# One tile list per expert, full tiles first, in an attention and top-2 expert kernel

## The chip, the cores and the metric

The kernel runs on one core of a Trainium2 chip. The metric is the device time of one execution in microseconds (us), the median of several runs. Engine names as in the profile: PE (TensorE), DVE (VectorE), ACT (ScalarE), POOL (GpSimd) and SP (SyncE, which here only issues DMAs).

## The reference, cut to what matters

```
x   = x + attention(layernorm(x), ctx)   # 16 batches x 128 rows, D = 128, 16 heads of 8, then Wo
h   = layernorm(x)                       # 2048 rows
p   = softmax(h @ wg.T)                  # 8 experts
w,i = top_k(p, 2);  w = w / sum(w)
y_e = (silu(h @ w1_e.T) * (h @ w3_e.T)) @ w2_e.T      # 256 hidden columns, fp32
out = x + sum over the two chosen experts of w * y_e
```

All is fp32. 2048 rows with two experts each make 4096 pairs (row, expert). How many pairs an expert gets is known only once the kernel has routed the rows.

## The kernel before, in words

The 16 batches are worked on in four quartets of four batches (512 rows). Attention of the quartets runs until about 180 us. As soon as the rows of a quartet are finished, they are normalised a second time and routed (`routing_step`, `place_rows` on DVE, small matmuls `fill(("x2T", q))`, `lg`, `rk`, `cn` on PE). `place_rows` writes into `rows_i` the place of every pair in a DRAM buffer `xg`, which has one region per expert. POOL then **sends** the quartet: eight indirect DMAs of 128 rows (L970, `send`), with the pair's number as a 129th column. A send waits for the send of the batch before it with the same k, so at most two are under way.

Then comes the expert stage, a loop over tiles of 128 pairs of one expert. For tile n, SP reads the rows from `xg` (L458, ring of XR = 15 buffers), PE turns them (L680), ACT and DVE split them into a high and a low part (L761, L1341), PE multiplies by w1 and w3 (`hidden`, L693 to L696), ACT and DVE make silu and product (L922, L1375), PE turns the result (L706), ACT and DVE split it (L761, L1346), PE multiplies by w2 (`down`, L719 and L720), DVE adds the two halves into `y_sb` (`take_rows`, L1353, ring of YR = 14), and POOL **scatters** the tile's rows to their pairs' places in the DRAM buffer `ys` (L1009). Every engine has its part of iteration n written out by hand in one fixed order, so an engine that waits holds up all that stands behind it in its own list. On PE and DVE the work of tile n + 1 (turning, split) stands ahead of `hidden(n)`, and `down` and `take_rows` come three iterations behind.

Which expert and which rows a tile has is read from a table `tab`, made on DVE (`table`) and loaded into registers by SP (`open_phase`, L441) and PE (`columns`, L730). The list of tiles has a fixed length, enough for the worst split. Rows between an expert's last pair and the end of its last tile are **pads**: nine DMAs of 128 rows (L435, L439) write them, and their number is out of range, so a scatter drops them.

There are two phases, each with its own regions, `ys` buffer, pads and table: quartets 0 to 2 with 31 tiles, and quartet 3 with 15. Phase 1 can't open until the last quartet has been routed, its table made and its eight sends landed. That happens inside the loop of phase 0: the last batch's heads in iterations 0 to 2, its statistics and normalisation in 3 and 4, routing on DVE in 8 to 11, the table in 13 to 15, and on POOL one send after every second scatter from n = 8 to 22. POOL's scatter n waits until scatter n - 2 has landed (up to n = 39).

SP's list in the loop: read n waits for the turning of tile n - 15 and for the landing of scatter n - 15; ahead of read 31 stands `open_phase(1)`. After the reads SP waits for all scatters of phase 0, brings the results of quartets 0 to 2 back (L468, six DMAs of 256 KB), waits for those of phase 1, brings back the last quartet (L475, four of 128 KB), and writes the output. DVE's `gather` (L1362, L1363) weighs the two results of each row and adds them to x; gathers 0 to 5 stand in the last six tile iterations, 6 to 15 after the loop.

## Time and profile before

| | us |
|---|---|
| median of 3 runs (298.17 to 303.82) | 299.11 |
| the profiled execution, its own time | 301.1 |
| its span in the trace | 299.3 |
| PE busy (share of the span) | 225.5 (75%) |
| DVE busy | 219.7 (73%) |
| ACT busy | 139.2 (47%) |
| POOL busy | 114.3 (38%) |

Times inside the trace count from the start of the span. The profiled execution took 1.8 us more than its span, and 2.0 more than the median. A busy share is an average over attention and the expert stage, which have different limits; the chain of waits tells which wait ends last at each moment. POOL's busy time for a DMA is only the issuing (0.97 us for an indirect one); the transfer lands later.

### The profile page before, as it was taken

What the parts mean: (1) busy time and instruction counts of PE and PEld (TensorE: products, weight loads), DVE (VectorE), ACT (ScalarE), POOL (GpSimd) and SP (SyncE); (2) the same over time, 40 slices, a digit from 0 to 9 for tenths busy, and PEclk for the clock granted to TensorE, in tenths of its full rate; (3) what the DMA queues carried; (4) which work ended last, traced back from release to release, by engine and by line L of the source; (5) the groups of instructions that cost most, each with busy time, mean ns of one, the idle gap of its engine ahead of it and who ended that gap; (6) DMA issues with size and microseconds to landing.
All of it is one profiled execution on the core that took longest, in us unless ns stands there. A gap on an engine that the chain in (4) does not pass through costs nothing.

```text
span 299.3 us, 5642 instructions
## 1 busy us (share of the span) xinstructions
PE 225.5 (75%) x1522; PEld 171.6 (57%) x1522; DVE 219.7 (73%) x636; ACT 139.2 (47%) x312; POOL 114.3 (38%) x125
## 2 busy tenths in 40 slices
PE   0666888999899789795678664886889983999700
PEld 0643565667566557563366333775869973898500
DVE  5689965886688777969776831788788880788963
ACT  6684156655764474331445461543345550555300
POOL 5202150405030521053863540055367656443650
PEclk9996599999999999788557965999799996899965
DMA  7954513451344124426021333212123344253107
GB/s 214 339 189 99 132 29 79 94 115 34 70 98 82 35 47 93 83 59 208 10 63 45 68 76 83 58 31 73 37 68 88 81 84 102 64 157 103 37 11 211
DMA packets 40862, 27.31 MB, mean 91 GB/s; under 512 B 5214, under 2 KB 38501, under 8 KB 40448
## 3 DMA queue, kind: packets, MB, share of 16 engines
q1 hardware_dynamic: 37440, 20.95, 29.7%
q0 software_dynamic: 2816, 5.27, 5.9%
q10 hardware_dynamic: 576, 0.72, 0.8%
q8 instruction: 14, 0.23, 0.3%
q14 instruction: 16, 0.13, 0.2%
HBM read 13.27 MB, written 7.37 MB: 69 GB/s over the span
## 4 chain that ended last, share of the span: by engine, by line
PE 41%; DVE 22%; DMA 17%; SPq 8%; issue 7%; POOL 2%; ACT 1%; POOLq 1%; DVEq 0%
SPq L413 7%; PE bank L500 7%; DVE m_neg L1317 5%; DMA ys<-big 5%; DMA xg<-st_hi,rows_i 4%; DMA bd<-st 3%; PE bank L693 3%; PE bank L640 3%; PE bank L719 3%; PE bank L619 3%; PE bank L657 3%; PE bank L643 3%; PE bank L696 3%; PE bank L694 3%; PE bank L506 2%
## 5 line engine op out<-in xcount | busy, mean ns | idle before, releaser
L1009 POOL DMA_INDIRECT ys<-big x46 | 45.2, 982 | 38.3 <-DMA ys<-big 18.3
L1317 DVE TENSOR_REDUCE m_neg<-bank 128x4 f32<-128x512 f32 x64 | 43.3, 683 | 15.6 <-PE bank L657 15.2
L887 ACT ACTIVATE big<-bank 128x512 f32<-128x512 f32 x64 | 37.5, 597 | 23.5 <-PE bank L643 23.3
L761 ACT ACTIVATE st<-bank 128x128 fp32r<-128x128 f32 (+1 forms) x92 | 26.3, 329 | 35.3 <-PE bank L706 19.6
L970 POOL DMA_INDIRECT xg<-rows,rows_i x24 | 24.0, 1000 | 27.5 <-DVE rows_i L1173 12.4
L657 PE MATMUL bank<-bd,st 128*128 128x512 f32 x64 | 29.6, 499 | 6.4 <-DMA bd<-st 5.2
L640 PE MATMUL bank<-m_bd,ones_b 128*128 128x512 f32 x64 | 32.2, 504 | 2.4 <-ACT big L887 1.9
L1263 DVE SCALAR_TENSOR_TENSOR st<-st_hi,cst,bank 128x512 fp32r<-128x512 f32 x32 | 23.4, 748 | 9.2 <-ACT st_hi L761 4.5
L719 PE MATMUL bank<-bd,st 128*128 x92 | 27.5, 320 | 2.3 <-DVE big L1353 2.1
L987 POOL TENSOR_TENSOR m_bd<-mT,cst 128x512 fp32r<-128x512 f32 x16 | 17.2, 1109 | 30.1 <-DVE mT L1242 30.1
L922 ACT ACTIVATE big<-bank 128x256 f32<-128x256 f32 x46 | 17.7, 385 | 22.0 <-PE bank L696 21.8
L643 PE MATMUL bank<-bd,st 128*128 128x512 f32 x64 | 27.8, 434 | 0.0
L1375 DVE TENSOR_TENSOR big<-big,bank 128x256 f32<-128x256 f32 x46 | 19.3, 419 | 11.4 <-ACT big L922 11.2
L953 POOL TENSOR_SCALAR ve<-mv 128x4 f32<-128x4 f32 x8 | 1.8, 228 | 66.2 <-DVE mv L1040 66.2
L693 PE MATMUL bank<-bd,st 128*128 x46 | 23.7, 515 | 3.1 <-DVE st L1341 2.8
L720 PE MATMUL bank<-bd,st 128*128 x92 | 24.7, 290 | 0.0
L1341 DVE TENSOR_TENSOR st<-bank,st 128x128 fp32r<-128x128 f32 x46 | 13.0, 283 | 13.1 <-ACT st L761 12.9
L680 PE MATMUL bank<-cst,big 128*128 128x128 f32 x46 | 13.7, 298 | 11.0 <-DMA big<-xg 11.0
L657 PEld LDWEIGHTS bank<-bd,st 128*128 128x128 f32 x64 | 14.1, 227 | 13.7 <-issue 6.6
L1346 DVE TENSOR_TENSOR st<-bank,st 128x256 fp32r<-128x256 f32 x46 | 19.4, 422 | 2.7 <-ACT st L761 1.4
L719 PEld LDWEIGHTS bank<-bd,st 128*128 128x128 f32 x92 | 18.1, 197 | 5.1 <-issue 3.5
L1353 DVE TENSOR_REDUCE big<-bank 128x128 f32<-128x256 f32 x46 | 19.2, 418 | 1.2 <-PE bank L720 1.0
(159 smaller groups left out, 538.0 us busy)
## 6 DMA issues: line engine op xcount, KB each, us to landing
bd<-st SPq DMA_DIRECT2D x128, 64.0 KB, 2.0
big<-xg SPq DMA_DIRECT2D x46, 64.5 KB, 1.9
raw<-in_L_ffn_w SPq DMA_DIRECT2D x2, 1024.0 KB, 9.0
raw<-ys SPq DMA_DIRECT2D x6, 256.0 KB, 4.6
xg<-in_patterns SPq DMA_DIRECT2D x18, 64.5 KB, 3.4
x_all<-in_x SPq DMA_DIRECT2D x4, 256.0 KB, 3.9
rows<-in_mask_BxS_if POOLq DMA_DIRECT2D x4, 256.0 KB, 4.9
ctx_all<-in_L_ffn_w SPq DMA_DIRECT2D x1, 1024.0 KB, 6.0
```

The source lines that it names most:

```text
L640: nc.tensor.matmul(s2[k % 2][:, :], ones_b[:, b, :], m_bd[:, NJ * g:NJ * (g + 1), :].rearrange("p h q -> p (h q)"), start=True, stop=False)
L643: nc.tensor.matmul(s2[k % 2][:, :], st[:, (u - 1) % 2, 1, g, b * S:(b + 1) * S], bd_slot(0, n)[:, g, :, :].rearrange("p j q -> p (j q)"), ...
L657: nc.tensor.matmul(s1[k % s1_ring(u)][:, :], st[:, u % 2, 0, g, (b - 1) * S:b * S], bd_slot(1, n)[:, g, :, :].rearrange("p j q -> p (j q)" ...
L693: nc.tensor.matmul(both, t_lo[n % 2], first_high[:, :, bass.ds(col[n], I)], start=True, stop=False)
L719: nc.tensor.matmul(o, g_hi[n % GR][:, c * P:(c + 1) * P], w, start=(c == 0), stop=False)
L720: last = nc.tensor.matmul(o, g_lo[n % GR][:, c * P:(c + 1) * P], w, start=False, stop=(c == 1))
L761: return nc.scalar.activation(o, i, ACT.Copy)
L887: nc.scalar.activation(prob[n % 2][:, NJ * g:NJ * (g + 1), :].rearrange("p h q -> p (h q)"), s2[k % 2][:, :], ACT.Exp, scale=SCALE).then_i ...
L970: pool.indirect_dma_start(xg[f], bass.IndirectOffsetOnAxis(rows_i[:, n, k:k + 1], 0), sent_rows(n // QB)[:, n % QB, k, :], None, bounds_ch ...
L1009: pool.indirect_dma_start(ys[f], bass.IndirectOffsetOnAxis(xt[n % XR][:, D:RW].bitcast(I32), 0), y_sb[n % YR], None, bounds_check=2 * CAPS ...
L1263: nc.vector.scalar_tensor_tensor(st[:, u % 2, is_k, g, :], st_hi[:, n % SH, :].bitcast(F32), cst[:, (C_CK if is_k else C_CQ):(C_CK if is_k ...
L1317: nc.vector.tensor_reduce(m_neg[:, H * (b - 1) + NJ * g:H * (b - 1) + NJ * (g + 1)], s1[k % s1_ring(u)][:, :].rearrange("p (j q) -> p j q" ...
```

## The change

All four quartets go to one list per expert: one `xg` with one region per expert, one `ys`, one running count. The list has 39 tiles in all. A tile is full once 128 pairs of its expert are there; three quartets have 3072 pairs, of which at most 127 in each of 8 experts are left over, so at least 17 full tiles exist before the last quartet is routed. These 17 are the first part of the list (`full_tiles`). The other 22 (`other_tiles`) are in two groups per expert: first, expert by expert, the tiles that the first three quartets have begun and that are not among the 17, then the tiles that only the last quartet fills. The results of quartets 0 to 2 are complete after tile 31 (`FIRST_TILES`).

Moved: `open_phase(1)`, with the only nine pads that are left, stands ahead of read 17 on SP; the first opening has no pads. The last batch's heads and its statistics stand ahead of the loop; normalisation is in iteration 0, routing in 4 to 6 and 8, the second table in 10 to 12 (with twice as many groups). A fourth part of the first table is new on DVE (tick 15 of the last attention block). POOL sends the last quartet in one row after scatter 3. Scatter n waits for scatter n - 2 up to tile 16, for n - 4 from 17 on. All 16 gathers stand behind the loop.

```diff
@@ -55,12 +55,13 @@
 EPS = 1e-5
 SH = 3
 CT = 128
-PHASES = (3, NQ - 3)
-CAPS = [n * T for n in PHASES]
-NTS = [(2 * c - E) // CT + E for c in CAPS]
-NT = sum(NTS)
-NC = CAPS[0] // CT
-REGS = [c + CT for c in CAPS]
+ROUTED = 2 * (NQ - 1) * T
+FULL_TILES = (ROUTED - E * (CT - 1) + CT - 1) // CT
+FIRST_TILES = (ROUTED - E) // CT + E
+NT = (2 * B * S - E) // CT + E
+NTS = (FULL_TILES, NT - FULL_TILES)
+NC = B * S // CT
+REG = B * S + CT
...
-            def open_phase(f):
-
-                sp.wait_ge(pad_ready, f + 1)
-                sp.dma_start(xg[f][E * REGS[f]:E * REGS[f] + CT, :], consts[:, C_PAD:C_PAD + RW]).then_inc(padded[f], 16)
-                _, at = nc.values_load_multi_w_load_instructions(pad[0:1, f, :], [mybir.EngineType.SP], min_val=0, max_val=E * REGS[f] - CT,
+            def fill_pads():
+
+                sp.wait_ge(pad_ready, 1)
+                sp.dma_start(xg[E * REG:E * REG + CT, :], consts[:, C_PAD:C_PAD + RW]).then_inc(padded, 16)
+                _, at = nc.values_load_multi_w_load_instructions(pad[0:1, :], [mybir.EngineType.SP], min_val=0, max_val=E * REG - CT,
                                                                  skip_runtime_bounds_check_because=IN_RANGE)
                 for row in at:
-                    sp.dma_start(xg[f][bass.ds(row, CT), :], consts[:, C_PAD:C_PAD + RW]).then_inc(padded[f], 16)
+                    sp.dma_start(xg[bass.ds(row, CT), :], consts[:, C_PAD:C_PAD + RW]).then_inc(padded, 16)
+
+            def open_phase(f):
+
+                if f:
+                    fill_pads()
                 sp.wait_ge(tab_ready, f + 1)
-                _, at = nc.values_load_multi_w_load_instructions(tab[0:1, 0, 32 * f:32 * f + NTS[f]], [mybir.EngineType.SP],
-                                                                 min_val=0, max_val=E * REGS[f], skip_runtime_bounds_check_because=IN_RANGE)
+                _, at = nc.values_load_multi_w_load_instructions(tab[0:1, 0, NTS[0] * f:NTS[0] * f + NTS[f]], [mybir.EngineType.SP],
+                                                                 min_val=0, max_val=E * REG, skip_runtime_bounds_check_because=IN_RANGE)
                 for q in (range(3) if f == 0 else range(3, NQ)):
                     for k in range(2):
                         sp.wait_ge(sent[q][k], 16 * QB)
-                sp.wait_ge(padded[f], 16 * (E + 1))
+                if f:
+                    sp.wait_ge(padded, 16 * (E + 1))
                 return list(at)
 
             rows = open_phase(0)
             sp.wait_ge(o_full, 3 * QB)
             for n in range(NT):
-                f = int(n >= NTS[0])
                 if n == NTS[0]:
                     rows += open_phase(1)
                 if n >= XR:
...
-            results_back(0)
+            results_back(FIRST_TILES)
...
-            results_back(1)
+            results_back(NT)
...
+            heads_by_query(B - 1)
+            heads_by_dim(B - 1)
+            project_out(B - 1)
...
-                if n < 3:
-                    (heads_by_query, heads_by_dim, project_out)[n](B - 1)
-                if n == 5:
+                if n == 1:
                     fill(("x2T", NQ - 1))
-                if n == 7:
+                if n == 3:
                     fill(("lg", NQ - 1))
-                if n == 10:
+                if n == 6:
                     fill(("rk", NQ - 1))
-                if n == 12:
+                if n == 8:
                     fill(("cn", 1))
...
-                f = int(n >= NTS[0])
-                if 2 <= n < NT - 6:
-                    pool.wait_ge(ysb_out[(n - 2) % YR], 16 * ((n - 2) // YR + 1))
-                pool.indirect_dma_start(ys[f], bass.IndirectOffsetOnAxis(xt[n % XR][:, D:RW].bitcast(I32), 0), y_sb[n % YR], None,
-                                        bounds_check=2 * CAPS[f] - 1, oob_is_err=False).then_inc(ysb_out[n % YR], 16)
-                if n == 8:
-                    pool.wait_ge(rows_ready, NQ)
-                if 8 <= n < 8 + 4 * QB and n % 2 == 0:
-                    send(QB * (NQ - 1) + (n - 8) // 4, n // 2 % 2)
+                back = 2 if n < NTS[0] else 4
+                if n >= back:
+                    pool.wait_ge(ysb_out[(n - back) % YR], 16 * ((n - back) // YR + 1))
+                pool.indirect_dma_start(ys, bass.IndirectOffsetOnAxis(xt[n % XR][:, D:RW].bitcast(I32), 0), y_sb[n % YR], None,
+                                        bounds_check=PAIRS - 1, oob_is_err=False).then_inc(ysb_out[n % YR], 16)
+                if n == 3:
+                    send_quartet(NQ - 1)
...
+                if part == 3:
+                    own(nc.vector.tensor_tensor(until[:, :], until[:, :], tiles[:, :], ALU.subtract))
+                    own(nc.vector.tensor_scalar(until[:, :], until[:, :], -1.0, float(n), ALU.mult, ALU.add))
+                    own(nc.vector.scalar_tensor_tensor(tiles[:, :], until[:, :], 0.0, tiles[:, :], ALU.max, ALU.min))
+                    tiles_of(begun[:, :], 0, 3 * T // CT, ALU.is_gt)
+                    own(nc.vector.tensor_tensor(group[:, 0, :], begun[:, :], tiles[:, :], ALU.subtract))
+                    own(nc.vector.scalar_tensor_tensor(origin[:, 0:E], tiles[:, :], float(CT), base, ALU.mult, ALU.add))
+                    own(nc.vector.scalar_tensor_tensor(origin[:, E:2 * E], begun[:, :], float(CT), base, ALU.mult, ALU.add))
+
+            def other_tiles(part):
+
+                n = NTS[1]
+                number = cst[:, C_TILE:C_TILE + n]
+                groups = group[:, :, :].rearrange("p k e -> p (k e)")
+                below = x2s[1][:, 0:4 * E * E].rearrange("p (m f) -> p m f", f=2 * E)
+                passed, moved = (x2s[k][:, 0:n * 2 * E].rearrange("p (n m) -> p n m", m=2 * E) for k in range(2))
+                spot, column = (line[:, k * n:(k + 1) * n] for k in range(2))
+                if part == 0:
+                    counts(1)
+                    nc.vector.tensor_tensor(pad[:, :], cnt[:, :], base, ALU.add).then_inc(pad_ready, 1)
+                    tiles_of(tiles[:, :], 0, NC, ALU.is_gt)
+                    own(nc.vector.tensor_tensor(group[:, 1, :], tiles[:, :], begun[:, :], ALU.subtract))
+                    own(nc.vector.tensor_tensor(below, groups.unsqueeze(1).to_broadcast([P, 2 * E, 2 * E]), upto, ALU.mult))
+                    own(nc.vector.tensor_reduce(ended[:, 1:2 * E + 1], below, X, ALU.add))
+                if part == 1:
+                    own(nc.vector.scalar_tensor_tensor(origin[:, :], ended[:, :], -float(CT), origin[:, :], ALU.mult, ALU.add))
+                    own(nc.vector.tensor_tensor(step[:, :], origin[:, 1:2 * E + 1], origin[:, 0:2 * E], ALU.subtract))
+                    own(nc.vector.tensor_tensor(passed, ended[:, 1:2 * E + 1].unsqueeze(1).to_broadcast([P, n, 2 * E]),
+                                                number.unsqueeze(2).to_broadcast([P, n, 2 * E]), ALU.is_le))
+                    own(nc.vector.tensor_tensor(moved, passed, step[:, :].unsqueeze(1).to_broadcast([P, n, 2 * E]), ALU.mult))
+                    own(nc.vector.tensor_reduce(spot, moved, X, ALU.add))
+                if part == 2:
+                    own(nc.vector.tensor_tensor(moved, passed, cst[:, C_STEP:C_STEP + 2 * E].unsqueeze(1).to_broadcast([P, n, 2 * E]), ALU.mult))
+                    own(nc.vector.tensor_reduce(column, moved, X, ALU.add))
+                    own(nc.vector.tensor_copy(tab[:, 1, NTS[0]:NT], column))
+                    own(nc.vector.scalar_tensor_tensor(spot, number, float(CT), spot, ALU.mult, ALU.add))
+                    nc.vector.tensor_scalar(tab[:, 0, NTS[0]:NT], spot, origin[:, 0:1], float(E * REG), ALU.add, ALU.min).then_inc(tab_ready, 1)
...
-                                table(0, tick - 9)
+                                full_tiles(tick - 9)
                             if tick == 12:
                                 weigh(2)
+                            if tick == 15:
+                                full_tiles(3)
...
+            normalise_heads(B - 1)
+            take_projection(B - 1)
+            second_statistics(NQ - 1)
             rest_of_tile(0)
             for n in range(NT + 3):
                 if n + 1 < NT:
...
                 if n == 0:
-                    normalise_heads(B - 1)
-                if n == 2:
-                    take_projection(B - 1)
-                if n == 3:
-                    second_statistics(NQ - 1)
-                if n == 4:
                     normalise(QB * (NQ - 1), 2 * NQ - 1)
-                if 8 <= n < 11:
-                    routing_step(NQ - 1, n - 8)
-                if n == 11:
+                if 4 <= n < 6:
+                    routing_step(NQ - 1, n - 4)
+                if n == 6:
+                    routing_step(NQ - 1, 2)
+                if n == 8:
                     place_rows(NQ - 1)
-                if 13 <= n < 16:
-                    table(1, n - 13)
-                if NT - 5 <= n < NT + 1:
-                    gather(n - NT + 5)
-
-            for b in range(6, B):
+                if 10 <= n < 13:
+                    other_tiles(n - 10)
+
+            for b in range(B):
```

What the change moves, as lists of instructions per engine. First **POOL** in the expert stage, before: L1009 is a scatter (`ys<-big`), L970 a send (`xg<-rows,rows_i`).

```order
L954 TENSOR_TENSOR rstd<-ve,halves 128x4
L1009 DMA ys<-big 3072x128 x9
L970 DMA xg<-rows,rows_i 5248x129
L1009 DMA ys<-big 3072x128 x2
...
L1009 DMA ys<-big 3072x128 x8
L1009 DMA ys<-big 1024x128 x15
```

POOL now (L1019 scatters, L980 sends):

```order
L965 TENSOR_TENSOR rstd<-ve,halves 128x4
L1019 DMA ys<-big 4096x128 x4
L980 DMA xg<-rows,rows_i 17536x129 x8
L1019 DMA ys<-big 4096x128 x35
L172 UNCONDITIONAL_BRANCH
```

The eight sends were spread over scatters 8 to 22; they now stand together between scatters 3 and 4.

**DVE** ahead of the loop's first tiles, now (L1125 to L1119 heads of the last batch, L1043 and L1048 its statistics, L1066 and L1069 its normalisation, L1398, L1435 and L1403 tile work); before, the first rows were the tile work, and the others stood in iterations 0 to 4:

```order
L1125 RECIPROCAL rz<-bank 128x16
L1128 TENSOR_TENSOR on<-bank,rz 128x128
L1119 TENSOR_TENSOR x_all<-bank,x_all 128x128
L1043 BN_STATS stats<-x_all 128x6 x4
L1048 BN_AGGR mv<-stats 128x2 x4
L1398 TENSOR_TENSOR st<-bank,st 128x128 x2
L1435 TENSOR_TENSOR big<-big,bank 128x256
L1066 CAST rows<-cst 128x8
L1069 TENSOR_SCALAR rows<-x_all,mv,rstd 128x2x128 x4
L1398 TENSOR_TENSOR st<-bank,st 128x128
```

The heads and statistics now precede the split of tile 0, and the normalisation stands right behind the first product.

**DVE** at the end of the loop, before (L1353 adds up a tile's result, L1362 and L1363 are a gather):

```order
L1353 TENSOR_REDUCE big<-bank 128x128
L1346 TENSOR_TENSOR st<-bank,st 128x256
L1362 SCALAR_TENSOR_TENSOR big<-raw,wgt,x_all 128x128
L1363 SCALAR_TENSOR_TENSOR ctx_all<-raw,wgt,big 128x128
L1353 TENSOR_REDUCE big<-bank 128x128 x2
L1362 SCALAR_TENSOR_TENSOR big<-raw,wgt,x_all 128x128
```

and now (L1410 adds up, L1419 and L1420 are a gather):

```order
L1410 TENSOR_REDUCE big<-bank 128x128
L1403 TENSOR_TENSOR st<-bank,st 128x256
L1410 TENSOR_REDUCE big<-bank 128x128 x2
L1419 SCALAR_TENSOR_TENSOR big<-raw,wgt,x_all 128x128
L1420 SCALAR_TENSOR_TENSOR ctx_all<-raw,wgt,big 128x128
```

The six gathers that stood between tiles have moved behind the last tile.

## Rows read from the trace of the kernel before

**Rows 1.** The view of `ys`: scatters' durations (ns), POOL's idle (us, times), landings.

```profile
L1009 POOL DMA_INDIRECT ys<-big x46: 969/971/1193, 195.7 to 288.6; - x46
...
  issue: 6.7, 21
...
DMA to landing us min/median/max: 2.1/2.6/7.0
```

**Rows 2.** Chain of waits, 240 to 250 us: start, length, what.

```profile
240.85 4.05 DMA ys<-big
...
247.02 2.35 DMA xg<-rows,rows_i
...
249.56 1.90 DMA big<-xg
```

**Rows 3.** Timeline of PE: start, length, instruction, idle before it and releaser.

```profile
184.77 0.79 PE L693 MATMUL bank<-bd,st 128*128 x1
...
222.44 0.49 PE L693 MATMUL bank<-bd,st 128*128 x1 [0.61 <-DVE st L1341]
...
251.51 0.48 PE L680 MATMUL bank<-cst,big 128*128 128x128 f32 x1 [5.89 <-DMA big<-xg]
251.86 0.79 PE L693 MATMUL bank<-bd,st 128*128 x1
...
260.17 0.49 PE L693 MATMUL bank<-bd,st 128*128 x1
...
263.42 0.48 PE L693 MATMUL bank<-bd,st 128*128 x1
...
278.82 0.49 PE L693 MATMUL bank<-bd,st 128*128 x1
```

**Rows 4.** Chain of waits at the end.

```profile
288.61 2.10 DMA ys<-big
...
291.31 2.94 DMA raw<-ys
...
294.34 0.36 DVE big L1362
```

**Rows 5.** The third quartet's sends: first on POOL's timeline, two later in the chain.

```profile
165.04 1.26 POOL L970 DMA_INDIRECT xg<-st_hi,rows_i  x1 [2.13 <-DVE rows_i L1173]
...
168.46 4.40 DMA xg<-st_hi,rows_i
...
178.96 2.29 DMA xg<-st_hi,rows_i
```

**Rows 6.** SP's pads on its timeline; then register loads of SP and PE by source line.

```profile
236.10 5.45 SPq L439 DMA_DIRECT2D xg<-in_patterns  x8
...
L441 SPq TENSOR_LOAD <-tab x2: 1537/1974/2411, 173.5 to 241.6; - x2
L730 PEldq TENSOR_LOAD <-tab x2: 1723/2322/2922, 178.0 to 252.7; - x2
```

**Rows 7.** DVE's timeline: heads, normalisation, places and one table step.

```profile
178.66 0.29 DVE L1109 TENSOR_TENSOR x_all<-bank,x_all 128x128 f32<-128x128 f32 x1 [1.88 <-PE bank L530]
...
195.57 1.57 DVE L1061 TENSOR_SCALAR rows<-x_all,mv,rstd 128x256 f32<-128x256 f32 x4
...
215.04 0.25 DVE L1173 CAST rows_i<-m_hl 128x8 int32<-128x8 f32 x1
...
220.77 0.27 DVE L1206 TENSOR_TENSOR ck<-until,cst 128x120 f32<-128x120 f32 x1
```

**Rows 8.** POOL's timeline: scatters, with the idle time before each.

```profile
260.29 0.97 POOL L1009 DMA_INDIRECT ys<-big  x1 [0.96 <-DMA ys<-big]
...
263.49 0.97 POOL L1009 DMA_INDIRECT ys<-big  x1 [0.94 <-DMA ys<-big]
```

**Rows 9.** DVE's timeline after the loop: two gathers in succession.

```profile
288.03 0.35 DVE L1362 SCALAR_TENSOR_TENSOR big<-raw,wgt,x_all 128x128 f32<-128x128 f32 x1
...
288.68 0.35 DVE L1362 SCALAR_TENSOR_TENSOR big<-raw,wgt,x_all 128x128 f32<-128x128 f32 x1
```

More of the change, by code:

```diff
@@ L312, in program @@
         pad_ready = sem("pad_ready")
-        padded = [sem(f"padded{k}") for k in range(2)]
+        padded = sem("padded")
         in_t = [sem(f"in_t{k}") for k in range(XR)]
@@ L1182, in weigh, with counts @@
                 own(nc.vector.tensor_reduce(wgt[:, QB * q:QB * (q + 1), :], spread[:, :, :, :], X, ALU.add))
-            def table(f, part):
-                n = NTS[f]
-                upto = cst[:, C_UPTO:C_UPTO + E * E].rearrange("p (e f) -> p e f", e=E)
+            upto = cst[:, C_UPTO:C_UPTO + 4 * E * E].rearrange("p (m f) -> p m f", f=2 * E)
+            base = cst[:, C_BASE:C_BASE + E]
+            def counts(f):
+                full(("cn", f))
+                nc.vector.tensor_copy(cnt[:, :], work_bank(("cn", f))[:, 0:E]).then_inc(into_sbuf(("cn", f)), 1)
+                taken(dve, ("cn", f))
@@ new lines, in tiles_of, with full_tiles @@
+            def tiles_of(out_tiles, first, last, compare):
+                c = last - first
+                need = x2s[0][:, 0:E * c].rearrange("p (e f) -> p e f", e=E)
+                own(nc.vector.tensor_tensor(need, cnt[:, :].unsqueeze(2).to_broadcast([P, E, c]),
+                                            cst[:, C_FULL + first:C_FULL + last].unsqueeze(1).to_broadcast([P, E, c]), compare))
+                own(nc.vector.tensor_reduce(out_tiles, need, X, ALU.add))
+            def full_tiles(part):
+                n = NTS[0]
```

93 lines of the change are left out of this document (45 added, 48 removed).

## The prediction

> **What bounds the kernel now.** I read the windows of the second half first (everything up to about 180 us stays, but for one small piece), then the chain of waits, then PE, POOL, SP and DVE in order of time. The expert stage starts with tile 0 at 184.77 and ends its last tile's start at 278.82 [rows 3]: 94.05 us for 45 steps. Undisturbed, a step is (263.42 - 260.17) / 2 = 1.625 us [rows 3], so 45 steps are 73.1 and 21 us are something else. One piece is the 5.89 us in which PE waits for a read of phase 1 at 251.51, followed by matmuls of 0.79 instead of 0.49 us: from 251.86 to 260.17 four steps took 8.3 instead of 6.5, 1.8 more [rows 3]. The longer duration is the lower of the two clocks (1.2 for 2.4 GHz) after an idle PE. The chain shows what that wait was for: scatters and sends that wait for one another's landings (4.05, then the last send, 2.35), then the read (1.90) [rows 2]. The rest, 13 us, is the last quartet's heads, statistics, routing and table between the tiles. Behind tile 45 come 20.5 us: three iterations, POOL's remaining scatters until 288.61, a landing of 2.10, the results' way back (2.94), four gathers and the output from 294.34 to 299.3 [rows 4]. So the stage is bound by the tile loop, with POOL's queue behind it at both ends.
>
> **The change, part by part.** I follow landmarks in the time of this trace.
>
> *Start of tile 0.* Two edits pull against each other. The nine pads no longer run beside the third quartet's sends. These took 165.04 to 178.96 + 2.29 = 181.25, 16.2 us, with one landing of 4.40 [rows 5]; four rounds of 2.3 to 2.6 plus 0.8 to issue the next would be 13.6. Reads could start 2.6 earlier. Against that, heads and statistics of the last batch and PE's register load (between 1.7 and 2.9 [rows 6], 1.9 for 17) now stand ahead of tile 0. They can't start before batch 14 is taken at 178.66 [rows 7]; the fourth table part ahead of it (eight small operations, estimated at 1.8, some of it in idle time) moves that to about 180.2. Two short DVE operations, three on PE, one on ACT and DVE's addition, each 0.3 to 0.8, make about 2.7 (an estimate from such rows as the 0.29 at 178.66), and the register load 1.9, then the split of tile 0: 185.0, that is **+0.2**. Ends: -2.5 (all of it hidden) and +1.8 (the table part wholly exposed and nothing gained).
>
> *Last quartet's rows.* Before, normalisation ended at 195.57 + 1.57 = 197.1 and `rows_i` was written at 215.3 [rows 7], 18.2 later over seven iterations. Now there are eight: 19.8. Normalisation follows tile 0's product (about 2.4 behind 185.0) and takes 1.7, so it ends at 189.1 and the rows are there at **208.9**.
>
> *PE at the second opening.* Tiles 0 to 16 took 222.44 - 184.77 = 37.7 [rows 3]. Off goes the statistics' 1 us. The second table now is wholly ahead of tile 16, and bigger. An operation on 120 elements took 0.27, one on 256 a quarter of 1.57 [rows 7]; on 22 x 16 = 352 elements I take 0.5, times five, plus some fourteen small ones: 5.9 us for the three parts, about 2.2 more than stood ahead of tile 16 before. PE is ready for tile 16 at 185.0 + 37.7 + 1.2 = **223.9**; ahead of it stands the turning of tile 17.
>
> *Second opening.* It needs three things. The sends in a row: first issue 208.9 + 0.8, and a row of 16.2 like the third quartet's, which also had nine pads beside it: 225.9. The other end is 13.6 (223.3); I take the upper, since the pads are there again. The pads: ready at 212.5, 1.9 for the first and the registers, 5.45 for eight [rows 6], all issued at 219.9. The table: four iterations and 4.7 behind the rows, 220.1, and SP's load of 22 numbers, 1.9 (1.54 for 15, 2.41 for 31 [rows 6]): 222.0. The sends decide. Issue and landing of read 17, 0.4 and 1.9 [rows 2]: 228.2. **PE waits 4.3** instead of 5.9, in another place, and what the idle PE costs afterwards in clock stays at 1.8 [rows 3]; the other end for it is 0.
>
> *Last tile.* Tile 16 starts at 228.4; 22 steps of 1.625 and 1.8: tile 38 starts at **265.9**. So the stage up to the last tile's start is 80.9 instead of 94.05. Of these 13.1, seven steps fewer are 11.4, the shorter stall 1.6, statistics and bigger table -1.2; the remaining 1.3 are what stood between tiles behind tile 16 and no longer does, the end of the table and the gathers. On PE, scatters 4 to 16 also have to be landed for reads 19 to 31; at the paces below they are, with some 3 us to spare.
>
> *POOL.* Blocked by the sends, it issues scatter 4 at 223.6 + 1.3 = 224.9. With a wait two back the pace is (263.49 - 260.29) / 2 = 1.6 [rows 8]: scatter 17 at 245.7. From there four may be under way, so only issuing counts, 0.97 and 6.7 / 21 = 0.3 [rows 1]: 21 more end at 272.8. The six loads of results come in meanwhile; the worst landing before was 7.0 [rows 1]; with four outstanding this costs 7.0 + 0.8 - 5.1, 2.7 at most, 0 at least, and I take 0.7. Scatter 38 at 273.5, landed 275.8, 0.6 + 2.94 back [rows 4]: 279.3.
>
> *DVE.* Tile 38's result is added up some 5.3 behind its start, 271.2. Twelve gathers of 0.65 [rows 9] and the weights, 0.8, now follow instead of standing between tiles: 279.8. That is the later one, by a hair. Four gathers and the output, 299.3 - 294.34 = 5.0 [rows 4]: the span ends at **284.8**, 14.5 less.
>
> The profiled execution took 301.1, the median is 299.11; minus 14.5 they give 286.6 and 284.6. I say **285**.
>
> The Trainium skill's page "DMA: Bandwidth & Descriptors" (Anatomy of one DMA, SWDGE path) prices a DMA from GpSimd at 2.0 us and bytes over 436 GB/s, 2.15 for 64 KB; by that estimate the row of sends would be about 12.3 and the time that of the first rival. This trace's landings of 2.29, 2.35, 4.05 and 4.40 agree with it only where nothing else is under way.
>
> **Rivals.** *1, the stall nearly goes.* The row takes 13.6: read 17 lands at 225.6, PE idles 1.7 and keeps its clock. POOL's end is 2.6 earlier, the tiles' 4.4; POOL decides, 276.7 + 5.0 = 281.7, on the median **281.5**. For it: no scatters run beside the row. Against: the pads do. Chance 0.20.
>
> *2, the stall only moves.* If rows or sends come 3 to 6 us later (routing in the first, slow-clocked iterations, more landings like 4.40), each microsecond counts once, for PE and POOL alike: **288 to 291**. Chance 0.20.
>
> *3, DVE holds up POOL.* The first send of the third quartet took 1.26 instead of 0.97 [rows 1, 5], while DVE was busy. If all eight in the row did, beside DVE's new table, that is 8 x 0.29 = 2.3: **287**. For it: more two-input DVE work stands beside this row than before. Against: the median of the scatters, 0.971, issued amid DVE's tile work. Chance 0.08. The Trainium skill's page "SBUF — State Buffer" (Who interferes with whom) has the rule: a DVE instruction with two SBUF inputs and a GpSimd one that reads SBUF block each other.
>
> *4, slower: landings set POOL's pace.* In the row four landings follow one another, and with a wait two back each scatter costs half of landing + 0.8. One us more per landing costs 4 in the row and 6.2 in scatters 4 to 16, 10 us in all, with 3 us of slack to PE and none to the end. The gain is used up at landings 1.4 longer than I assume (3.8 for scatters, 4.5 for sends); at 2.1 longer it is **306**. For it: 4.05 and 4.40 occur [rows 2, 5]. Against: the median is 2.6 [rows 1], and they occurred beside pads. Chance 0.04; short of it, between 293 and 305, 0.08.
>
> That the list does not open early is excluded by the code: `open_phase(1)` stands ahead of read 17, and 17 is what three quartets guarantee.
>
> **How the numbers follow.** My forecast, 282.5 to 288, has 0.40. What a measurement can tell is about 2%, 6 us: faster is below 293.1, slower above 305.1. Faster: 0.40 + 0.20 + 0.20 + 0.08 = 0.88; within 2%: 0.08; slower: 0.04. The range of 8 in 10 reaches from rival 1 with the start's lower end to rival 2's upper end, **279 to 291**.
>
> **What would show it.** Right: 39 tiles; eight sends in a row for some 16 us from about 209; one idle of PE of some 4 us ahead of tile 16 and none later; the last scatter within 1 us of the last gather before the results' wait. The start is wrong if tile 0 is not near 185; the rows' landmark if `rows_i` is not near 209; the POOL part if reads 19 to 31 make PE wait, or if DVE waits over 1 us for the last results. The whole is wrong if POOL's scatters end after 278.

## The result and the profile after

| | before | after |
|---|---|---|
| median, us | 298.97 (four runs, 298.17 to 303.82) | 290.14 (four runs, 289.75 to 291.26) |
| profiled execution: time, span | 301.1, 299.3 | 290.28, 288.5 |
| tile 0, tile 16, last tile (PE) | 184.77, -, 278.82 | 186.91, 230.20, 268.14 |
| idle PE at the second opening | 5.89 | 3.20 |

The ratio is 0.972 (95% interval 0.968 to 0.976): 8.8 us faster, where 14 were forecast. The time lies inside the range of 279 to 291, at its upper end, and outside the forecast's own 282.5 to 288. The profile after was taken on a run at its median; the one before on a run 2.1 us above it. So 10.8 us of span are 8.8 of median. Here and below, medians are of all runs of a set, while ratios and intervals leave out its slow runs (more than 1.5% above the fastest of their kernel), so the two can differ a little.

PE's timeline, which answers to [rows 3] (start, length, instruction, idle before it and releaser):

```profile
185.69 0.66 PE L691 MATMUL bank<-cst,big 128*128 128x128 f32 x2 [3.71 <-issue]
186.91 0.79 PE L704 MATMUL bank<-bd,st 128*128 x1 [0.56 <-DVE st L1398]
...
217.17 0.49 PE L704 MATMUL bank<-bd,st 128*128 x1 [1.64 <-DVE st L1398]
220.53 0.49 PE L704 MATMUL bank<-bd,st 128*128 x1 [1.53 <-DVE st L1398]
223.40 0.49 PE L704 MATMUL bank<-bd,st 128*128 x1 [1.04 <-DVE st L1398]
...
229.97 0.48 PE L691 MATMUL bank<-cst,big 128*128 128x128 f32 x1 [3.20 <-DMA big<-xg]
230.20 0.79 PE L704 MATMUL bank<-bd,st 128*128 x1
```

Two things are new. Ahead of tile 0 PE is idle for 3.71 us for "issue", so for nothing that another engine owes it. And tiles 12 to 14 wait for DVE, which makes the bigger table meanwhile; that cost nothing here, since the idle time ahead of tile 16 follows. The source lines of the register loads say what the issue was (they answer to [rows 6]; durations in ns, then first and last start):

```profile
L452 SPq TENSOR_LOAD <-tab x2: 1492/3114/4736, 169.9 to 223.1; - x2
...
L744 PEldq TENSOR_LOAD <-tab x2: 1883/3062/4240, 181.4 to 231.1; - x2
```

PE's load of 17 numbers at 181.4 took 4.24 us, its load of 22 at 231.1 only 1.88; on SP it is the load of 22 that was long, 4.74. On the chain of waits the first shows as issue behind read 0's landing, the second by its name:

```profile
180.66 1.84 DMA big<-xg
182.51 3.18 issue
185.69 0.46 PE bank L691
...
222.84 0.25 DVE tab L1271
223.10 4.74 SPq L452
228.13 1.79 DMA big<-xg
229.97 0.48 PE bank L691
```

POOL's row of sends (it answers to [rows 5]), and the scatter behind it:

```profile
211.65 0.96 POOL L980 DMA_INDIRECT xg<-rows,rows_i  x1 [7.33 <-DVE rows_i L1183]
...
220.65 0.97 POOL L980 DMA_INDIRECT xg<-rows,rows_i  x1 [1.71 <-DMA xg<-rows,rows_i]
224.14 0.97 POOL L980 DMA_INDIRECT xg<-rows,rows_i  x1 [2.51 <-DMA xg<-rows,rows_i]
225.47 0.97 POOL L980 DMA_INDIRECT xg<-rows,rows_i  x1 [0.36 <-issue]
226.74 0.97 POOL L1019 DMA_INDIRECT ys<-big  x1 [0.30 <-issue]
```

First to last issue is 13.82 us; in the other runs read 17 is issued 2.5 us behind the last send (but for the seven more tiles below, where SP's load is longer still), which here would be 227.95. SP's load ended at 227.84: a tie. The end, which answers to [rows 4, 9], on DVE and on POOL:

```profile
274.65 0.42 DVE L1410 TENSOR_REDUCE big<-bank 128x128 f32<-128x256 f32 x1 [1.48 <-PE bank L731]
275.00 0.34 DVE L1419 SCALAR_TENSOR_TENSOR big<-raw,wgt,x_all 128x128 f32<-128x128 f32 x1
...
283.26 0.22 DVE L1192 TENSOR_REDUCE wgt<-spread 128x8 f32<-128x64 f32 x1
283.51 0.35 DVE L1419 SCALAR_TENSOR_TENSOR big<-raw,wgt,x_all 128x128 f32<-128x128 f32 x1
```

```profile
274.43 0.97 POOL L1019 DMA_INDIRECT ys<-big  x1 [0.95 <-DMA ys<-big]
276.52 0.97 POOL L1019 DMA_INDIRECT ys<-big  x1 [1.12 <-DMA ys<-big]
```

DVE goes from the last sum to the last gather without a gap; it no longer waits for results. POOL has caught up with the tiles: its last scatter leaves 1.45 us behind the end of the last sum (275.07), and the profile puts the wait ahead of it down to the landing of an earlier scatter.

### The profile page after: what moved, and what is told of

Same layout as the page of the kernel before. It is cut to its first block, busy times and chain, and to the rows that moved or that the text cites. A ratio compares the mean times of both kernels' runs of the same rounds, so it can differ in the third digit from the quotient of the medians.

```text
span 288.5 us, 5277 instructions
## 1 busy us (share of the span) xinstructions
PE 214.9 (75%) x1445; PEld 162.2 (56%) x1445; DVE 214.6 (74%) x619; ACT 132.5 (46%) x291; POOL 107.7 (37%) x118
## 4 chain that ended last, share of the span: by engine, by line
PE 49%; DVE 27%; DMA 9%; issue 7%; SPq 4%; ACT 2%; POOL 1%; DVEq 0%; POOLq 0%; ACTq 0%
PE bank L511 7%; DVE m_neg L1374 5%; PE bank L630 4%; PE bank L730 4%; PE bank L651 4%; DMA xg<-st_hi,rows_i 4%; PE bank L668 4%; PE bank L654 3%; PE bank L704 3%; PE bank L707 3%; DMA bd<-st 3%; PE bank L731 3%; PE bank L517 3%; PE bank L705 3%; SPq L419 2%
## 5 line engine op out<-in xcount | busy, mean ns | idle before, releaser
L1374 DVE TENSOR_REDUCE m_neg<-bank 128x4 f32<-128x512 f32 x64 | 43.4, 684 | 15.7 <-PE bank L668 15.5
L1019 POOL DMA_INDIRECT ys<-big x39 | 38.2, 980 | 32.1 <-DVE big L1410 15.8
L899 ACT ACTIVATE big<-bank 128x512 f32<-128x512 f32 x64 | 37.5, 597 | 24.2 <-PE bank L654 24.0
L980 POOL DMA_INDIRECT xg<-rows,rows_i x24 | 23.9, 996 | 39.3 <-DVE rows_i L1183 18.9
L773 ACT ACTIVATE st<-bank 128x128 fp32r<-128x128 f32 (+1 forms) x78 | 22.5, 329 | 32.0 <-PE bank L717 16.8
L1435 DVE TENSOR_TENSOR big<-big,bank 128x256 f32<-128x256 f32 x39 | 16.3, 419 | 12.1 <-ACT big L935 12.1
L730 PE MATMUL bank<-bd,st 128*128 x78 | 23.8, 324 | 1.9 <-DVE big L1410 1.9
L935 ACT ACTIVATE big<-bank 128x256 f32<-128x256 f32 x39 | 15.0, 386 | 21.2 <-PE bank L707 21.0
L704 PE MATMUL bank<-bd,st 128*128 x39 | 20.2, 519 | 5.3 <-DVE st L1398 5.3
L668 PEld LDWEIGHTS bank<-bd,st 128*128 128x128 f32 x64 | 14.1, 228 | 13.9 <-issue 6.9
L731 PE MATMUL bank<-bd,st 128*128 x78 | 21.7, 297 | 0.0
L651 PEld LDWEIGHTS bank<-m_bd,ones_b 128*128 128x128 f32 x64 | 13.9, 218 | 10.2 <-issue 5.9
L630 PE MATMUL bank<-big 128*32 128x128 f32 x512 | 19.2, 296 | 0.0
L1403 DVE TENSOR_TENSOR st<-bank,st 128x256 fp32r<-128x256 f32 x39 | 16.5, 422 | 3.4 <-ACT st L773 2.5
L730 PEld LDWEIGHTS bank<-bd,st 128*128 128x128 f32 x78 | 15.9, 204 | 4.5 <-issue 3.5
L1410 DVE TENSOR_REDUCE big<-bank 128x128 f32<-128x256 f32 x39 | 16.3, 418 | 2.5 <-PE bank L731 2.4
```

Source lines behind the costliest of these rows:

```text
L630: last = nc.tensor.matmul(ob[n % 2][R * j:R * (j + 1), half * P:(half + 1) * P], va[(n // QB) % 2][:, ((n % QB) * 4 + half * 2 + i) * NJ + ...
L651: nc.tensor.matmul(s2[k % 2][:, :], ones_b[:, b, :], m_bd[:, NJ * g:NJ * (g + 1), :].rearrange("p h q -> p (h q)"), start=True, stop=False)
L668: nc.tensor.matmul(s1[k % s1_ring(u)][:, :], st[:, u % 2, 0, g, (b - 1) * S:b * S], bd_slot(1, n)[:, g, :, :].rearrange("p j q -> p (j q)" ...
L704: nc.tensor.matmul(both, t_lo[n % 2], first_high[:, :, bass.ds(col[n], I)], start=True, stop=False)
L730: nc.tensor.matmul(o, g_hi[n % GR][:, c * P:(c + 1) * P], w, start=(c == 0), stop=False)
L731: last = nc.tensor.matmul(o, g_lo[n % GR][:, c * P:(c + 1) * P], w, start=False, stop=(c == 1))
```

## The experiments

The sets of four ran on three chips, on which the kernel before took 299.35, 311.74 and 301.25 us; so each run is compared with its own set, by ratio to the kernel before, or by landmarks of its trace.

### What a tile costs: seven more

```
-NT = (2 * B * S - E) // CT + E
+NT = (2 * B * S - E) // CT + E + 7
```

> The changed kernel with NT raised by 7, so that the list has 46 tiles again; the seven extra ones hold no rows. Theory A (the tile loop bounds the stage): seven steps of 1.62 us and a table of 29 instead of 22 columns (+0.4 us on VectorE) come on top: 290.1 + 11.8 = 301.9 us, tile 16 at +0.4. Rival B (GpSimd's queue bounds the second half): the extra scatters cost its undisturbed pace, 1.28 us each, 290.1 + 9.0 = 299.1 us. Rival C (full tiles cost more than empty ones because of their transfers): under 297 us.

Measured 311.07 us, ratio 1.040 (1.034 to 1.046): 20.8 us more, far over each theory. The loads show why:

```profile
L744 PEldq TENSOR_LOAD <-tab x2: 4238/5720/7203, 182.3 to 233.9; - x2
```

29 numbers took PE 7.20 us between tiles 16 and 17, and SP 6.10. On PE that is 8.4 us from tile 16 to tile 17 instead of 3.1, 5.3 more. On SP the load ended at 230.6, and read 17, issued at 230.94, came 2.3 later than the last send (226.13) and its 2.5 would have let it. More tiles make a longer row of `tab`, so its second row starts elsewhere. I wrote the bytes from the start of `tab` beside every load so far. Long: 156 and 184 (17 numbers, 4.24 and 4.24), 68 (22 and 29, 4.74 and 6.10), 252 (29, 7.20). Short: 0, 128, 192, 224 and 320 (15 to 31 numbers, 1.5 to 2.9, all loads of the kernel before among them). So before the change every load of `tab` began on a multiple of 32 bytes from its start, and after it two of four don't.

### The start: load ahead, and the old schedule

```
+            col = columns(0)
             heads_by_query(B - 1)
             heads_by_dim(B - 1)
             project_out(B - 1)
...
-            col = columns(0)
             turn_tile(0)
```

> TensorE loads its 17 registers ahead of the last batch's heads (about 178.9 us) instead of behind them (181.4). Theory A (the 4.24 us come from what runs beside the load, SyncE's fifteen reads being issued from 180.66): here it takes 1.5 to 1.9 us, tile 0 starts near 184.6 instead of 186.9 and the time is 287.8 us. Rival B (a load of 17 numbers takes TensorE over 4 us by itself): the heads come 4.2 us later, tile 0 stays near 187, 290.1 us or up to 1 us more.

Measured 289.54 us, ratio 0.970 (0.963 to 0.976); the load took 4.32 us from 178.2, 2.3 us before the first read was issued (180.54), and tile 0 started at 187.51. Rival B: the reads beside it are not the cause. Nor is the count alone, as the table's layout shows below.

The second experiment puts `heads_by_query`, `heads_by_dim` and `project_out` back into iterations 0 to 2 and the rest of the last quartet into those of the kernel before (cut to two of the moved parts):

```
-                if n == 8:
+                if n == 11:
                     place_rows(NQ - 1)
-                if 10 <= n < 13:
-                    other_tiles(n - 10)
+                if 13 <= n < 16:
+                    other_tiles(n - 13)
```

> The list of 39 tiles and everything else of the changed kernel, but the last quartet's heads, statistics, routing and table at the iterations they had before (heads in 0 to 2, normalisation in 4, routing 8 to 10, rows in 11, table 13 to 15). Theory A: tile 0 starts 2 to 3 us earlier (near 184.3), the rows three iterations later (4.9) less that start, so rows near 213 and the idle time ahead of tile 16 near 5.5 instead of 3.2 us; 290.1 + 2.2 = 292.3 us. Rival B (the start is all that counts, the second opening has room): 287.5 us. Rival C (the table's end stands ahead of tile 16 and everything slips): 295 us or more.

Measured 293.77 us, ratio 0.982 (0.980 to 0.984). Tile 0 at 184.36, as expected: there the long load (4.34 us, from 178.7) is over at 183.0, about when read 0 has landed. But the first send came at 217.50 instead of 211.65, and PE then waited 11.45 us ahead of tile 16, at 235.85, where 5.5 were expected. Theory A had the start right and the rows 3.7 us too early (near 213, measured 216.7); the time lies between A and C. So the earlier schedule of the change is worth 3.0 us by the ratios (3.6 by the medians), through the rows.

### The row of sends, moved

```
-                if n == 3:
+                if n == 9:
                     send_quartet(NQ - 1)
```

> The row of the last quartet's eight sends stands behind scatter 9 instead of scatter 3; GpSimd waited 7.33 us for rows_i ahead of the row, and scatters 4 to 9 fit in there. Theory A (behind the row GpSimd has slack; its last scatter waits for the last tile's result): no change, 290.1 us within 0.6, while the scatters' backlog behind the row ends some 8 us earlier. Rival B (the backlog of scatters holds reads or the results' way back): 287 to 288 us. Rival C (a landing of scatter 8 or 9 delays the first send): the idle time ahead of tile 16 grows by 1 to 1.3 us, 291.3 us.

Measured 297.67 us, ratio 0.995 (0.990 to 0.999): none of the three. I had not looked when scatter 9 can be issued: it needs tile 9's result. It went out at 223.33, so the row began 12.95 us later and tile 16 started 9.83 later. That is the clearest miss among my expectations, and the clearest proof that the row sets tile 16; that `rows_i` sets the row is shown by the experiment ahead of this one. The difference, 3, is the row itself. In this run the pads were over before it, on SP and POOL:

```profile
218.01 6.11 SPq L445 DMA_DIRECT2D xg<-in_patterns  x8
```

```profile
224.60 0.97 POOL L980 DMA_INDIRECT xg<-rows,rows_i  x1 [0.30 <-issue]
...
235.52 0.97 POOL L980 DMA_INDIRECT xg<-rows,rows_i  x1 [0.57 <-issue]
```

10.92 us from first to last issue instead of 13.82, so the pads beside the row are put at 2.9. Only this run has the last quartet's row without them, but the twelve other traces of the new list, all with pads beside it, have 12.67 to 14.24. The third quartet's row, which lost its pads by the change, went from 13.92 to 11.91.

### The table's layout alone

```
-        tab = sb("tab", [P, 2, NT], I32)
+        tab = sb("tab", [P, 2, 64], I32)
...
-tab[0:1, 1, NTS[0] * f:NTS[0] * f + NTS[f]]
+tab[0:1, 1, 32 * f:32 * f + NTS[f]]
```

(Parts of the changed lines; the same for row 0 and where DVE writes it.)

> Only the layout of the table tab changes: rows of 64 words, the second list from word 32, so that each of the four register loads begins at a multiple of 128 bytes from the start of tab; before this edit they begin at bytes 0 (17 numbers, 1.49 us), 68 (22 numbers, 4.74), 156 (17, 4.24) and 224 (22, 1.88). Theory A (where a register load begins sets its price, about 0.07 us a number on such a boundary and 0.21 to 0.25 off it): SyncE's second load takes 1.9 us, TensorE's first one 1.5 to 1.8; tile 0 starts near 184.6 instead of 186.9; behind the second opening the sends' landing decides in place of the load, and the shift of the start stays: 290.1 - 2.3 = 287.8 us. Rival B (the loads are long through what runs beside them, reads being issued at one, sends at the other): they stay at 4.2 and 4.7 us, and the time at 290.1. Rival C (the loads get short, but the row of sends holds everything): tile 0 earlier, idle time ahead of tile 16 longer by as much, 290.1.

Measured 295.55 us on the chip that took 311.74 for the kernel before: ratio 0.950 (0.937 to 0.962). Source lines, then PE:

```profile
L452 SPq TENSOR_LOAD <-tab x2: 1495/1558/1622, 169.6 to 219.7; - x2
...
L744 PEldq TENSOR_LOAD <-tab x2: 1566/1724/1883, 181.1 to 228.0; - x2
```

```profile
226.88 0.48 PE L691 MATMUL bank<-cst,big 128*128 128x128 f32 x1 [3.49 <-DMA big<-xg]
227.07 0.79 PE L704 MATMUL bank<-bd,st 128*128 x1
```

4.24 became 1.57 and 4.74 became 1.62, with as many numbers loaded at the same places in the program. Tile 0 started at 183.91 (3.0 earlier) and tile 16 at 227.07 (3.1 earlier). At the second opening the chain now goes through the last send (222.62) and its landing, so SP's shorter load brings nothing of its own. Theory A holds by the loads and by tiles 0 and 16, with a start 0.7 better than expected. From tile 16 to tile 38 this trace took 46.9 us instead of 37.9, so it ran once more on another chip:

> The aligned kernel once more, on another chip, since the chip of its first timing gave 311.7 us for the kernel before instead of 299. In that trace TensorE's first load took 1.57 and SyncE's second 1.62 us, tile 0 started at 183.91 instead of 186.91 and tile 16 at 227.07 instead of 230.20. Theory A (these 3.0 to 3.1 us stay to the end): 290.1 - 3.1 = 287.0 us, ratio to the kernel before 0.960. Rival B (from tile 17 on transfers set the pace, 1.72 us a step in that trace, and take the gain back): 289 us or more, steps over 1.65 us on this chip too.

Measured 286.51 us, ratio 0.951 (0.946 to 0.956), clear of the changed kernel's 0.968 to 0.976. Loads 1.56 and 1.63, tile 0 at 185.98 with read 0 issued 1.8 later than in the profile after (180.66); from read 0's issue to tile 0 it is 3.5 instead of 6.3. Tile 16 started at 228.45, 1.75 earlier than in the profile after, and from there to tile 38 it took 38.0. By the ratios this version beats both kernels, and it is 14.7 us under the 301.25 of its own set. Theory A was nearest, but its ratio of 0.960 lies above the interval: between 0.972 and 0.951 are some 6 us, of which the landmarks show about half, and the rest has no cause on record. The "1.72 us a step" of my expectation was misread: the first trace's steps were about 1.6, but for a few behind gaps, told of at the end.

### Where a load may begin

```
+            for first, count in ((0, 17), (1, 17), (2, 17), (4, 17), (8, 17), (16, 17), (0, 8), (1, 8), (0, 30), (3, 29)):
+                nc.values_load_multi_w_load_instructions(tab[0:1, 1, first:first + count], ...)
```

> The aligned kernel, with ten more register loads on TensorE behind its last product, whose values nobody uses: 17 numbers from words 0, 1, 2, 4, 8 and 16 of a row of tab, 8 numbers from words 0 and 1, 30 from word 0 and 29 from word 3. Theory A (the start address decides): 17 numbers take 1.5 to 1.9 us from words 0, 8 and 16 and about 4.2 from words 1, 2 and 4; 8 numbers 0.6 and 2.0; 30 from word 0 2.3 to 2.9 and 29 from word 3 about 7. Rival B (number and neighbours decide): equal counts take equal times here, where nothing else runs. Rival C (some other boundary, of 8 or 16 bytes): word 2 or 4 are short too.

It told nothing of this: the ten loads do not appear in the trace, presumably removed because nobody uses them. One run of the aligned kernel remains, 286.23 us. Which boundary counts stays open: all short starts, 224 among them, are multiples of 16 and of 32, and the four long ones of neither (184 is a multiple of 8, so 8 is not enough).

### Seven more tiles, aligned

The edit of the first experiment on the aligned kernel.

> The aligned table, and 46 tiles, of which seven hold no rows. Theory A (the price of a tile is a step of the loop; the 21 us that seven more tiles cost without alignment were for a half TensorE's load of 29 numbers, 7.20 us, and SyncE's, 6.10): both second loads take 2.2 to 2.9 us, and the time is that of the aligned kernel + 7 x 1.62 + 0.5 for the bigger table = 299.7 us. Rival B (tiles without rows cost 2 to 3 us each): 305 us or more.

Measured 307.74 us beside the aligned kernel's 295.55 in the same set (ratios 0.996 and 0.950): 12.2 us by the medians, 11.7 by the spans (305.6 and 293.9), and 14 give or take 4 by the ratios. In the traces, which both have the gaps told of at the end, tile 16 to the last tile is 58.5 us instead of 46.9: 11.6 for seven tiles. Theory A, by the traces: seven steps and little else; the ratios alone would allow rival B's 2 us a tile. The loads took 2.00 and 2.26. So of the 20.8 us of the first experiment some 8 to 9 were loads by this difference; its own trace shows 7.6 of them (5.3 on PE, 2.3 on SP).

### The end: gathers back into the loop, and the scatters' wait

```
+                if n >= NT:
+                    gather(2 * (n - NT))
+                    gather(2 * (n - NT) + 1)
...
-            for b in range(B):
+            for b in range(6, B):
```

> The aligned table, and gathers 0 to 5 in the three iterations behind the last tile, where VectorE has little to do, instead of behind the loop. Theory A (a tie at the end: VectorE would be done 3.9 us earlier, but the last results land only about when it is done now): 0.5 us less than the aligned kernel, 287.3, and VectorE then waits 2 to 3.5 us for the results' landing. Rival B (VectorE's chain alone sets the end): 3 us less or more, 284.8. Rival C (the gathers wait for the first results and hold up the last sums of tiles): 1 us more, 288.8.

Measured 294.68 us, ratio 0.952 (0.945 to 0.959), no difference from the aligned kernel beside it that these runs can tell. DVE waited 0.29 us for the last results, not 2 to 3.5: from the last tile's start to its sum it was 7.4 us instead of 6.1 (274.34 to 281.70, and 273.99 to 280.04), and the last scatter waits for that sum. So C's mechanism, at a price that the shorter end pays for: what VectorE wins behind the loop it takes from the tiles' sums.

```
-                back = 2 if n < NTS[0] else 4
+                back = 2
```

> The aligned table, and each scatter waits for the one two back throughout, as in tiles 0 to 16. Theory A (the loop is no faster than such a pace of about 1.6 us a scatter): the backlog of the row is never made up, and the last scatter comes 0.5 to 2 us later: 288.3 to 289.8 us. Rival B (landings grow in the second list and the wait sets GpSimd's end): scatters at 1.8 us or more, 292 us or later. Rival C (fewer transfers at once land sooner, and nothing is lost): 287.8 us or less.

Measured 296.26 us, ratio 0.959 (0.954 to 0.965): above the aligned kernel by 0.7 us in the medians, inside A, and by 3 in the ratios, whose intervals overlap. The trace says B. This run had no such gaps as the aligned kernel's on that chip: tile 38 started at 267.23 instead of 273.99, and the last sum at 273.34. The scatters did not follow. From 223.82 to 284.84 they took (284.84 - 223.82) / 34 = 1.8 us each, the last one 11.5 us behind the start of the last sum (1.4 in the aligned kernel), and DVE waited for the results:

```profile
290.14 0.35 DVE L1419 SCALAR_TENSOR_TENSOR big<-raw,wgt,x_all 128x128 f32<-128x128 f32 x1 [6.26 <-DMA raw<-ys]
```

With a wait two back POOL sets the end; by this row, `back = 4` in the second list is worth some 6 us of the change. The times of the pair don't show it; in the two traces the gaps delayed only the other one, and whether that holds for the runs without a trace is not known.

### Two further edits

Both runs have the aligned table and the gathers in the loop. The first moves a part of the first table as well:

```
-                            if tick == 15:
-                                full_tiles(3)
...
+                if n == 2:
+                    full_tiles(3)
```

> The aligned kernel, gathers 0 to 5 in the three iterations behind the last tile, and the fourth part of the first table (1.75 us on VectorE ahead of the last heads) moved into iteration 2 of the tile loop. Theory A (the part stood on the way to tile 0, but only 1.3 us of it: 'on' of batch 14 at 177.25 instead of 175.90): tile 0 and all behind it 1.3 us earlier, the gathers another 0.5 to 0.7: 287.0 - 2.0 = 285.0 us. Rival B (tile 0 waits for read 0 at about 182.5 and its turning instead): tile 0 at 183.6, 286 us. Rival C (in iteration 2 the part delays routing by as much): rows no earlier, 286.5 us.

Measured 288.07 us, ratio 0.959 (0.953 to 0.965), not better than the aligned kernel's 286.51 (0.951). From read 0's issue to tile 0 it is 3.54 us, as without the edit (3.53), so the table part did not stand on the way; and from tile 0 to the first send it is 25.4 instead of 24.5. Rival C.

The second moves routing forward (cut to two of the moved parts):

```
-                if n == 6:
+                if n == 5:
                     routing_step(NQ - 1, 2)
...
-                if n == 8:
+                if n == 7:
                     place_rows(NQ - 1)
```

> The same three edits, and the last quartet's second and third routing step, its ranks, rows and table each one iteration earlier (rows in 7 instead of 8, table in 9 to 11 instead of 10 to 12). Theory A (the row of sends starts with rows_i and sets read 17; a microsecond there is a microsecond of the end as long as TensorE idles ahead of tile 16): one early iteration, 1.6 to 2.3 us, off that idle time, 285.0 - 1.9 = 283.1 us. Rival B (TensorE has no idle time left, tile 16 waits for tile 15): 284.5 us. Rival C (routing steps in one iteration delay the tiles by what they win): 285.0 us.

Measured 287.0 us, ratio 0.958 (0.952 to 0.963). The intervals of this and the last overlap; in the traces tile 16 comes 2.0 earlier (226.08 for 228.09) and PE's idle time ahead of it falls from 3.03 to:

```profile
225.84 0.33 PE L691 MATMUL bank<-cst,big 128*128 128x128 f32 x1 [0.35 <-DMA big<-xg]
```

The spans are 283.4 and 285.6. A by the traces, unsettled by the times: neither of the two runs is faster than the aligned kernel by them.

This trace shows one thing more. PE hardly idled ahead of tile 16 and kept its clock (0.49 us a matmul), and still tile 17 started 3.08 us behind tile 16 instead of 1.6:

```profile
229.16 0.49 PE L704 MATMUL bank<-bd,st 128*128 x1 [1.32 <-DVE st L1396]
```

DVE's part of tile 17 was done at 226.8. What stands between the two tiles in PE's list is its second register load, here from 226.9 for 1.92 us, so until 228.8, with tile 17 0.3 behind it. In the profile after it ends at 233.0 and tile 17 starts at 233.25, in the run with seven more tiles at 241.1 and 241.41. So even an aligned load of 22 numbers cost some 1.5 us in this run. Moving it to where PE waits anyway was not tried.

## Why the prediction was right, step by step

The class and the range held; the time was 5 us too low. It fell into the band of rival 2 (288 to 291), which had its own conditions: rows or sends 3 to 6 us late. `rows_i` and tile 16 were 1.9 and 1.8 us late, from a cause the prediction did not have. So that the range held its upper end owes something to luck. In the trace's own time the span ended at 288.5 instead of 284.8; 2 more are the profile before.

- **Start of tile 0**: predicted 185.0, measured 186.91. The step that failed is "the register load 1.9": it took 4.24. The four loads of before [rows 6] could not show it, since all began on a boundary; I took their length for a matter of count alone. Two smaller errors nearly cancelled: the load began at 181.4, some 1.5 us earlier than the sum has it, and turning and splitting tile 0 behind it took 1.2 (185.69 to 186.91), where the sum leaves 0.2. The sends took 14.6 instead of 13.6, with no cost, because read 0 (landed 182.5) then waited for the load.
- **Last quartet's rows**: predicted 23.9 behind tile 0, measured 23.9 (210.84). Right.
- **Second opening**: the row with its landing 16.2, as taken from [rows 5]; the fourth experiment shows why that end of the bounds was the right one, 2.9 us of it for pads. The Trainium skill's page "DMA: Bandwidth & Descriptors" (Anatomy of one DMA, SWDGE path) gave 12.3 by my estimate; the row without pads beside it took 10.92 and a landing of about 2.3, 13.2, so it is near without pads and 3 us low with them. SP's load was costed at 1.9 and took 4.74, an error that the tie with the sends hid. PE's idle time was 3.2 instead of 4.3, because the table held tiles 12 to 14 for 4.2 us in all. From tile 0 to 16: 43.4 predicted, 43.3 measured.
- **Tiles 16 to 38**: 37.5 predicted, 37.9 measured. The size of the 1.8 us in it was about right (2.2 measured), its cause only in part: I put it all down to the clock behind an idle PE. With 0.35 us idle and the clock kept, the last experiment still took 36.9, so about 1 us in the profile after is the clock and the rest the register load between tiles 16 and 17. The lower end of 0 for this term could not have come out. Seven tiles fewer at 1.625 are 11.4; the traces of the pair of 39 and 46 gave 11.6.
- **The drain**: the last sum ended 6.9 behind the last tile's start instead of 5.3, the second error, 1.6 us. The 5.3 stands on no row, and the trace of before would have given 6.7: its last sum started at 285.1 and took 0.42, with the last tile at 278.82. What is left is 0.2 us. At the very end the last matmuls took 0.42 where those of 272.44 took 0.28, and DVE waited 1.48 for PE. Then twelve gathers and the weights, 8.4 for 8.6, and 5.0 to the end, as predicted.
- **POOL**: the pace from 245 us on was 1.28, as put (0.97 + 0.3); its last scatter left at 276.52 instead of 273.5, since the tile's result was there only at 275.07 and a landing was waited for behind it (1.12 of idle time). That it could take that pace is what kept DVE the last: with two back throughout it is 1.8 us a scatter and POOL the last by 6.26.
- **Rivals**: the stall neither went nor grew. DVE did not lengthen the sends of the row, 0.96 to 0.98 each.

The row of the kernel before for the drain (all 46 sums; shortest, median and longest in ns, then first and last start):

```profile
L1353 DVE TENSOR_REDUCE big<-bank x46: 413/418/425, 191.8 to 285.1; 128x128 f32<-128x256 f32 x46
```

Alignment gives back 3.0 to 3.1 us at tile 0 and tile 16 in its first trace (0.4 of them from an earlier read 0), and 0.9 and 1.75 in its second, where read 0 came 1.8 late; counted from read 0's issue it is 2.6 and 2.7. The aligned kernel's 14.7 below its kernel before is the forecast's size. That the rest of the difference (drain 1.6, the profile before 2) has gone in that set is not shown: there chips and runs differ by as much.

## What to carry to other kernels

Cost a register load by where it begins, not by its count alone, and lay such a table out so that each part begins on a boundary (32 bytes was enough here), whatever its length. Look at what stands behind the load in its engine's list: even a short one is a wait there. A shorter list is worth its steps only if nothing of its making slides in front of the first one. When two things end together, such as a load and a landing, or gathers and a last scatter, an experiment on one of them shows little in the time, and the trace has to say which is next.

## What the runs showed of the hardware

| start of the load, bytes from `tab` | 15 | 17 | 22 | 29 | 31 numbers |
|---|---|---|---|---|---|
| multiple of 32 | 1.54, 1.72 | 1.48 to 1.57 | 1.62 to 2.05 | 2.00, 2.26 | 2.41, 2.92 |
| 68, 156, 184, 252 | - | 4.22 to 4.34 | 4.62 to 4.76 | 6.10, 7.20 | - |

The table has all loads of `tab` in the fourteen traces. A `TENSOR_LOAD` of int32 numbers from SBUF into registers took 0.07 to 0.12 us a number on a multiple of 32 bytes and 0.21 (all on SP) to 0.26 (all on PE) off it. What ran beside it differed from trace to trace and moved neither row into the other. Eight numbers of another array, `pad`, also from a multiple of 32 bytes, took 0.54 to 0.55 us in every trace, but for one load of 1.01 in the trace of before (at 166.4); why is open. The Trainium skill's page "Runtime: NRT & Kernel Launch" (Instruction fetch mechanics) gives about 200 ns a register for loads from HBM; these come from SBUF, and the second row is near that figure, the first at about half of it or less.

The same kernel before took 299, 301 and 312 us on three chips, and in the aligned kernel's trace the third was not slower evenly or by its mean clock (0.872 there, 0.856 in the profile after): from tile 0 to 16 it took 43.2 us, as in the profile after (43.3). PE's timeline shows where most of its 9 us between tiles 16 and 38 lay:

```profile
246.75 0.38 PE L730 MATMUL bank<-bd,st 128*128 x1 [1.85 <-issue]
249.71 0.79 PE L704 MATMUL bank<-bd,st 128*128 x1 [1.90 <-issue]
```

These are gaps for which no releaser is found, together 3.75 us; the two steps behind them, with matmuls at the lower clock, took 3.70 and 2.77 instead of 1.6. The run with gathers in the loop had the gaps in the same place (1.65 and 2.30), and the one with 46 tiles a single one of 3.90 there, put down to DVE; the one with `back = 2` had none. What makes them was not tried, and the kernel before has no trace on that chip.
